# Decoder layer with a mixture of experts on one core: second expert weights read in place by TensorE, gate quotients, pads and tile transposes moved

## The reference, cut to what matters

```python
x = x + self_attention(layernorm(x))            # 16 heads of 8, window of 32, rotary
x = x + cross_attention(layernorm(x), ctx)      # 16 heads of 8, window of 16, with biases
x = x + experts(layernorm(x))

def experts(x):                                 # E = 8 experts, F = 512, top 2
    probs = softmax(x @ gate_w)
    topw, topi = top_k(probs, 2)
    topw = topw / topw.sum(-1)                  # so: w0 = 1 / (1 + q), w1 = q / (1 + q), q = exp(l1 - l0)
    out = 0
    for e in range(8):
        out += combine[:, e] * (gelu(x @ w1[e]) @ w2[e])
    return out
```

## Time and profile before

| what | value |
|---|---|
| median of 3 runs | 527.29 us (526.48 to 527.38) |
| the profiled execution, its own time | 529.45 us |
| its span, first to last instruction | 527.3 us |
| mean granted TensorE clock | 0.989 |
| busy: TensorE, its weight loads | 473.5 us (90%), 381.6 us (72%) |
| busy: VectorE, ScalarE, GpSimd | 363.3 us (69%), 358.0 us (68%), 307.5 us (58%) |

### The profile page before, as it was taken

The page is one execution under the profiler, slowest core; times in us unless marked ns, Lnnn a source line. Parts: engine busy times, 40 slices in busy tenths (PEclk is TensorE's granted clock), DMA queues, the critical chain, the costliest instruction groups (busy, mean ns, idle before and its releaser), DMA issues.

```text
span 527.3 us, 29060 instructions
## 1 busy us (share of the span) xinstructions
PE 473.5 (90%) x11117; PEld 381.6 (72%) x11117; DVE 363.3 (69%) x1271; ACT 358.0 (68%) x1051; POOL 307.5 (58%) x415
## 2 busy tenths in 40 slices
PE   2599999999998989998999999898978999999991
PEld 1276767767776667776777776666977899999991
DVE  5377888888886745777877878987656444444863
ACT  3376777778776768787888888777544466665651
POOL 2444445454453535387787787676777455555662
PEclk9999999999999999999999999999999899999996
DMA  8311111111111100011101111121223222227273
GB/s 233 98 57 51 51 49 60 50 50 60 46 53 44 29 14 18 14 35 44 38 30 41 36 33 47 34 60 45 54 67 104 77 73 72 71 71 270 59 208 112
DMA packets 40966, 35.03 MB, mean 66 GB/s; under 512 B 6445, under 2 KB 37295, under 8 KB 40896
## 3 DMA queue, kind: packets, MB, share of 16 engines
q1 hardware_dynamic: 35712, 24.69, 16.4%
q0 software_dynamic: 4320, 8.53, 4.9%
q10 hardware_dynamic: 864, 0.86, 0.6%
HBM read 18.63 MB, written 11.68 MB: 58 GB/s over the span
## 4 chain that ended last, share of the span: by engine, by line
PE 74%; DVE 6%; issue 6%; DMA 5%; POOL 3%; SPq 2%; ACT 2%; DVEq 1%; POOLq 0%; ACTq 0%
PE p_probsT L634 10%; PE p_scores L1230 8%; PE p_att_bank L624 8%; PE p_scores L517 8%; PE p_scores L562 5%; PE p_qk L1239 4%; PE p_v_bank L587 4%; PE p_probsT L1239 4%; PE p_scores L511 4%; PE p_att_bank L572 3%; PE p_qk L529 3%; PE p_qk L538 2%; PE p_v_bank L603 2%; PE p_att_bank L941 2%; DMA got<-sent_rows 2%
## 5 line engine op out<-in xcount | busy, mean ns | idle before, releaser
L763 POOL TENSOR_TENSOR k_heads<-qk,consts 128x512 f32<-128x512 f32 x64 | 67.0, 1047 | 86.8 <-DVE qk L825 56.1
L1298 POOL DMA_INDIRECT expert_results<-weighted,result_at x71 | 74.1, 1044 | 52.0 <-ACT weighted L1264 39.1
L864 DVE TENSOR_REDUCE shift<-p_scores 128x8 bf16<-128x512 f32 (+1 forms) x128 | 74.0, 618 | 24.9 <-PE p_scores L517 24.7
L661 ACT COPY probsT<-p_probsT 128x512 f32<-128x512 f32 x128 | 75.6, 591 | 21.1 <-PE p_probsT L634 20.9
L1230 PE MATMUL p_scores<-gotT,w_now 128*128 128x128 f32 x568 | 76.8, 279 | 4.9 <-issue 2.8
L634 PE MATMUL p_probsT<-consts,probs 128*128 128x128 f32 x512 | 78.7, 276 | 0.0
L667 ACT ACTIVATE probs<-p_scores 128x512 f32<-128x512 f32 x128 | 77.9, 609 | 0.1
L1009 POOL DMA_INDIRECT sent_rows<-row,slot_u x64 | 65.6, 1025 | 16.6 <-issue 14.6
L1230 PEld LDWEIGHTS p_scores<-gotT,w_now 128*128 128x128 f32 x568 | 69.7, 193 | 6.6 <-ACT gotT L1256 3.4
L720 ACT COPY values<-p_v_bank 32x128 f32<-32x128 f32 x256 | 68.4, 267 | 2.3
L1253 ACT ACTIVATE hidden<-p_scores 128x512 f32<-128x512 f32 x71 | 42.4, 597 | 32.7 <-PE p_scores L1230 32.7
(11 more groups left out here) (160 smaller groups left out, 924.3 us busy)
## 6 DMA issues: line engine op xcount, KB each, us to landing
got<-sent_rows SPq DMA_DIRECT2D x71, 66.0 KB, 1.9
swapped<-raw SPq DMA_DIRECT2D x64, 64.0 KB, 1.9
w<-w_in SPq DMA_DIRECT2D x32, 128.0 KB, 2.3
back<-expert_results SPq DMA_DIRECT2D x7, 512.0 KB, 6.1
ctxT<-ctxT_in SPq DMA_DIRECT2D x32, 64.0 KB, 2.0
x<-x_in SPq DMA_DIRECT2D x4, 448.0 KB, 9.5
out<-x SPq DMA_DIRECT2D x7, 256.0 KB
expert_results<-weighted,result_at POOLq DMA_INDIRECT x71, 2.3
```

The lines of the kernel that those rows point to most:

```text
L661: nc.scalar.copy(probsT[:, 4 * half:4 * half + 4, :], p_probsT[:, :].rearrange("p (m q) -> p m q", q=P)).then_inc(s_pT, 1)
L763: nc.gpsimd.tensor_tensor(k_heads[:, :, BLK:], qk[:, 1:2, :].to_broadcast([P, G, P]), cv(C_HEAD, G).unsqueeze(2).to_broadcast([P, G, P]), ...
L864: nc.vector.tensor_reduce(shift[:, half * 8:half * 8 + 8], p_scores[:, half * 8:half * 8 + 8, low:WIN], AX.X, ALU.max).then_inc(s_max, 1)
L1298: nc.gpsimd.indirect_dma_start(out=results, out_offset=bass.IndirectOffsetOnAxis(ap=result_at[:, slot:slot + 1], axis=0), in_=weighted[:, ...
```

## The change

Four edits in one. (1) `w2_now` and its 71 copies on VectorE go; TensorE loads the block's place from the table into a register of its own (`col`, ahead of the wait for gelu) and reads the second weights from `w2` at that address. It waits for the weights and the early table ahead of the first block and for the late table ahead of block 20. (2) In `pe_step` the two row transposes stand in front of the values' projection. (3) GpSimd makes the quotients of the last two pairs earlier: that of tiles 28 and 29 ahead of tile 27's sends, that of tiles 30 and 31 between the sends of tiles 28 and 29; for that the last sends are split into a piece per tile. (4) SyncE sends the pads one by one, each behind one of the reads of blocks 18 to 25.

```diff
@@ SyncE
             for c in range(PADS_AT):
                 read_rows(sp, 0, c)
-            send_pads(sp, range(E))
             for c in range(PADS_AT, EARLY):
                 read_rows(sp, 0, c)
+                if c - PADS_AT < E:
+                    send_pads(sp, (c - PADS_AT,))
@@ pe_step
                 yield
+                if runs(h, c, 2) or runs(h, c, 3 + ahead) or (not own and runs(h, c, -2)):
+                    v_bank_read()
+                if not own and runs(h, c, -2):
+
+                    n = at(-2)
+                    nc.tensor.wait_ge(s_xn3, n + 1)
+                    nc.tensor.transpose(p_x3T, xn3[:, (c - 2) % 4, :], ident).then_inc(s_x3Traw, 1)
+                if runs(h, c, 3 + ahead):
+
+                    n = count(3 + ahead)
+                    nc.tensor.wait_ge(s_xn, n + 1)
+                    nc.tensor.transpose(p_xT, xn[:, (c + 3 + ahead) % 2, :], ident).then_inc(s_xTraw, 1)
                 if runs(h, c, 2):
 
-                    v_bank_read()
                     src = xnT[:, (c + 2) % 2, :] if own else ctxT[:, (c + 2) % 2, :]
...
                     mm.then_inc(s_vraw, 1)
-                if not own and runs(h, c, -2):
-
-                    n = at(-2)
-                    if not runs(h, c, 2):
-                        v_bank_read()
-                    nc.tensor.wait_ge(s_xn3, n + 1)
-                    nc.tensor.transpose(p_x3T, xn3[:, (c - 2) % 4, :], ident).then_inc(s_x3Traw, 1)
-                if runs(h, c, 3 + ahead):
-
-                    n = count(3 + ahead)
-                    if not runs(h, c, 2):
-                        v_bank_read()
-                    nc.tensor.wait_ge(s_xn, n + 1)
-                    nc.tensor.transpose(p_xT, xn[:, (c + 3 + ahead) % 2, :], ident).then_inc(s_xTraw, 1)
@@ pool_step
                 if not own and isinstance(h, int) and c in LAST_SENDS:
-
-                    route_pool(h, c, LAST_SENDS[c])
+                    for tile in LAST_SENDS[c]:
+                        yield
+                        route_pool(h, c, [tile])
@@ expert_pe
-        def expert_pe(h, c, _):
+        def expert_pe(h, c, cols):
             n = U * h + c
+
+            def col(lead):
+                if c + lead not in cols:
+                    cols[c + lead] = nc.tensor.value_load(table_at(0, n + lead), min_val=0, max_val=(E - 1) * F)
+                return cols[c + lead]
...
             if block_there(h, c, -1):
                 half = (c - 1) % 2
+                at = col(-1)
                 nc.tensor.wait_ge(s_gelu, n)
-                nc.tensor.wait_ge(s_w2_now, n)
                 wait(nc.tensor, s_y, n - 2)
                 for f in range(FC):
-                    mm = nc.tensor.matmul(p_y[half], hidden[:, half, f * P:(f + 1) * P], w2_now[:, half, f * P:(f + 1) * P],
+                    mm = nc.tensor.matmul(p_y[half], hidden[:, half, f * P:(f + 1) * P], w2[:, bass.ds(at + f * P, P)],
                                           start=(f == 0), stop=(f == FC - 1))
@@ expert_dve
-            if block_there(h, c, 1):
-                at = col(1)
-                wait(nc.vector, s_down, n)
-                nc.vector.tensor_copy(w2_now[:, (c + 1) % 2, :], w2[:, bass.ds(at, F)]).then_inc(s_w2_now, 1)
@@ TensorE's program
             pe.wait_ge(s_probs, 4 * B)
+            pe.wait_ge(s_moe_w, 16 * B)
+            pe.wait_ge(s_tab, 1)
+            cols = {}
             for c in (-2, -1, 0):
-                expert_pe(0, c, None)
+                expert_pe(0, c, cols)
...
             table_pe()
+            pe.wait_ge(s_tab, 2)
             expert_steps(pe, expert_pe, 20)
@@ GpSimd's program
             expert_pool(0, 2, None)
+            go(steps[B], 3)
+            ratio_pool(B)
             go(steps[B], ALL)
-            ratio_pool(B)
             expert_pool(0, 3, None)
             expert_pool(0, 4, None)
+            go(steps[B + 1], 4)
+            ratio_pool(B + 2)
             go(steps[B + 1], ALL)
             expert_pool(0, 5, None)
-            ratio_pool(B + 2)
```

More of the change, by code:

```diff
@@ L233, in build @@
         w1_now = sb("w1_now", [P, 2, F])
-        w2_now = sb("w2_now", [P, 2, F])
         gotT = sb("gotT", [P, 2, P])
@@ L278, in build @@
         s_gTraw, s_gT, s_up, s_gelu = sem("gotT_in_psum"), sem("gotT_made"), sem("hidden_in_psum"), sem("hidden_made")
-        s_w1_now, s_w2_now, s_down, s_y = sem("w1_copied"), sem("w2_copied"), sem("y_in_psum"), sem("y_weighted")
+        s_w1_now, s_down, s_y = sem("w1_copied"), sem("y_in_psum"), sem("y_weighted")
         s_read = [sem(f"results_read{i}") for i in range(len(PARTS))]
@@ L1315, in _ @@
             pe.wait_ge(s_probs, 4 * B)
+            pe.wait_ge(s_moe_w, 16 * B)
+            pe.wait_ge(s_tab, 1)
+            cols = {}
             for c in (-2, -1, 0):
-                expert_pe(0, c, None)
+                expert_pe(0, c, cols)
             go(steps[B - 1], ALL)
-            expert_pe(0, 1, None)
+            expert_pe(0, 1, cols)
             go(steps[B], 3)
-            expert_pe(0, 2, None)
+            expert_pe(0, 2, cols)
             go(steps[B], ALL)
-            expert_pe(0, 3, None)
-            expert_pe(0, 4, None)
+            expert_pe(0, 3, cols)
+            expert_pe(0, 4, cols)
             go(steps[B + 1], ALL)
-            expert_pe(0, 5, None)
-            expert_pe(0, 6, None)
+            expert_pe(0, 5, cols)
+            expert_pe(0, 6, cols)
             go(steps[B + 2], ALL)
-            expert_pe(0, 7, None)
-            expert_pe(0, 8, None)
+            expert_pe(0, 7, cols)
+            expert_pe(0, 8, cols)
             go(steps[B + 3], ALL)
             for c in range(9, 20):
-                expert_pe(0, c, None)
+                expert_pe(0, c, cols)
             table_pe()
+            pe.wait_ge(s_tab, 2)
             expert_steps(pe, expert_pe, 20)
```

## The result

The changed kernel took 522.09 us (median of 4 runs, 518.97 to 522.45) against 527.34 us: a ratio of 0.988 (95% interval 0.984 to 0.992). Measured again later, beside a kernel before of 529.6 us, it took 520.44 us, a ratio of 0.983 (0.979 to 0.987). So it is faster, by some 5 to 9 us, where 17.8 were forecast. The profiled execution took 522.17 us; its span is 520.3.

The account below looks back on a forecast made before the run. TensorE was taken as the bound, busy nine tenths of the span. Savings of 5.8 + 5.0 + 3.3 + 4.2 - 0.5 = 17.8 us took the profiled 529.45 to 511.7, less 2.2 for the median: 509.5 us, range 504 to 526.

Parts of the forecast that it names:

- Transposes: In attention, moving them ahead of the values' projection saves 5.8 us in self tiles and 5.0 us in cross tiles.
- (a) to (c): In attention: L624's wait for ScalarE's copy, 0.08 us; VectorE's wait for scores; transposes' wait for normalised rows, 0.1 us.
- 0.18: Saving in us per self tile from the moved transposes, after L624's wait for ScalarE's copy.
- Wait (a): In a self tile, L624's second half waits for ScalarE's copy of the turned probabilities, about 0.08 us.
- Rival 3: The moved transposes save nothing, as another wait takes their place: 7.0 us left, 520 us; 0.10 together with Rival 4.
- Quotients and pads: Around the first expert blocks, earlier quotients save 3.3 us and pads spread between reads save 4.2 us.
- Both holes: TensorE's waits of 1.17 and 2.12 us before the hidden matmuls at 383.97 and 394.12 close: 3.3 us.
- Second weights in place: In the expert blocks, 0 per block; the wait for the late table ahead of block 20 costs 0.5 us once.
- x: Extra cost of a register operand per second-weights matmul; taken at the near end, nothing, with far end 0.56 us per block.
- rivals 1 and 2: TensorE's sequencer bounds expert blocks: partly, 515 to 526 us, chance 0.18; or slower than before, 545 us, chance 0.09.
- The 526 us: In expert blocks, if firmware decodes register-operand matmuls: 0.26 us per block, about 16 us over the blocks.
- Rival 4: Quotients and pads save little, as VectorE's late table steps end as late: 517 us; 0.10 together with Rival 3.

Follow-up runs that it names:

- split wait: Changed kernel with L511's wait for ScalarE's exponents split, its first two matmuls waiting for the first half only: 515.03 us, ratio 0.976.
- 64 instructions ahead: Changed kernel with 64 empty instructions at the start of TensorE's program: 515.14 us; the same without the moved transposes: 518.58 us.
- split wait and shift: Changed kernel with L511's wait for ScalarE's exponents split and 64 empty instructions at the start of TensorE's program: 511.03 us, ratio 0.968.

## Why the prediction was wrong, by its steps

**Transposes: the step that failed.** The segment went as worked out: L621 stands 0.28 us behind the values' start, as in the tile of the earlier trace rows. Of what may take that back I weighed three waits, (a) to (c), and missed a fourth, which stands a line further: L511 of the next tile, which waits for ScalarE's second exponent. In the kernel before it had 0.02 us to spare, and the trace of before had it: that exponent follows the copy of the earlier trace rows and ends at 85.96, L511 started at 86.13, 0.17 us later, and the hand-over alone takes 0.15, as the tiles of the kernel after show, where L511 waits for it. With the split wait the tile takes 4.63 us, less even than the 4.67 forecast; so the 0.18 was real, and hidden. (Wait (a), put at 0.08 us, took about 0.05: from the output to the next tile's first matmul it is then 0.76 us, where it was 0.71.) What was left: 0.02 us per plain self tile, 0.24 in each of five tiles at the turn of the loop, and 22.11 - 21.45 = 0.66 us per four tiles of the cross loop (0.16 each, 0.22 forecast). With the 64 instructions ahead that is 3.4 us of 10.8.

A second miss was of another kind. I counted the holes of "issue" as given, because no instruction was added. But the place of a wait changes when the next piece of code is asked for, and in the first turn of the self loop alone 3.2 us went in the profile, clock included. By itself the move cost 2 us; on top of the other parts it cost 2 us by the first measurement (0.988 against 0.984) and nothing by the second (0.983). Rival 3 (the transposes save nothing, 520 us) named the effect, but not either cause; that it came to within 2 us of the result is luck in part, since the 7.0 us that it left for the other parts were too few, and the move lost where it put nothing.

**Quotients and pads: right, and too small.** The quotients came at the times forecast (shifted by the 2.9 us lost ahead: 377.3 and 386.3, forecast 378 and 387). Both holes and that of the pads closed, and the clock stayed up. 9.4 us were won to block 21, where 3.3 + 4.2 - 0.5 = 7.0 were put down. The two moves alone gave 7.5 us there, as much as the two terms; what came on top was the copies. The terms had the missing copies of VectorE only as a help to close the two holes; the runs put 1.9 us on them on top of the two moves, which leave holes ahead of blocks 16 and 17 without them. Alone they are worth 1.7 us in one profile and nothing in the time.

**Second weights in place: right.** A block takes 1.895 us with the register operand as without, so x is at the near end, and rivals 1 and 2 fall. The 526 us were an estimate from the Trainium skill (TensorE: Matmul & The Clock Gate, "Wait — 56ns, not 53.3ns?"), for the case that the firmware decodes such matmuls. L1242's eight in 0.89 us, back to back, give no sign of it.

**Rival 4 falls.** Quotients and pads gave 0.989 alone.

**The sum** of what the runs show: 9.4 us won behind the attention, 2.9 lost in it, 6.5 in the profiled execution to block 21 (7.0 in all); by the medians 5 to 9. A slip of the sum: with every tile at its full 0.26 and no cost of the table the lower end of the range is 505.4 us, not 504. The 511.0 us of the kernel with split wait and shift lie near the forecast of 509.5, but by two things that the change does not contain.

## What to carry to other kernels

An engine's next wait must be looked for past the edited piece: follow the bound engine to its next instruction with a releaser, and write down how late that releaser ends. What is to spare is the time from that end to the start, less the hand-over (0.15 us here, read where the wait binds); 0.02 us of slack took all but a tenth of a saving of 0.2 us in each tile. Splitting the wait by what each instruction really overwrites gave it back. Where code runs once (unrolled steps, a loop's first turn), look for holes of "issue" at fixed distances in instructions: a moved wait can lengthen them, and a difference of one per cent between two orders may be theirs and not that of the order, which pairs of kernels with and without some empty instructions ahead tell apart.

## What the runs showed of the hardware

- TensorE's code arrives in packets of 16 KB. At the end of one TensorE stood for up to 2.69 us, even in the middle of a run of matmuls that wait for nothing. Behind some such holes (2.27 us in the changed kernel, 2.00 with the transposes alone, 0.88 with 64 instructions ahead) a stretch of 4 us has a granted clock of 0.57; behind others (2.27 us with the split wait, and again with the transposes moved in the loops alone) it stayed at 1.00.
- 64 empty instructions were worth 4 to 7 us in one kernel and nothing clear in two others, and 128 cost 10.6 us at the start.
- In 12 of 19 profiled executions the second tile took 5.9 to 7.0 us, in the others 4.73. From 24.6 to 28 us the matmuls took 1.6 times as long, which is their pace where the granted clock is 0.57 (timeline of the kernel after, second tile and the stretch from 49.5 us):

```profile
25.14 1.16 PE L517 MATMUL p_scores<-k_heads,qk 32*32 32x256 f32 x32
...
50.27 1.15 PE L517 MATMUL p_scores<-k_heads,qk 32*32 32x256 f32 x32
```

The windows' column shows 1.00 for the second tile, but the trace has no record of the granted clock ahead of 29.12 us there. In the twelve slow executions the first record comes 3.2 to 6.5 us after the second tile's start, and the matmuls are fast from about then on; in the seven others it comes before that start. So, by that pace, TensorE ran at its lower level until then, and the 1.6 us of the 2.9 that the profiled attention lost are the clock's. The first tile is as slow in all 19 (L517 1.16 us). Why the clock rises later in some executions stays open: it occurs with the transposes in either order; in the changed kernel both profiles have it, in the kernel before the one has not.
- Eight matmuls with a register address in their moving operand take as long as with a fixed one, 0.89 us.
